# Gated cross-attention and routed experts on one core: Q and K as stacked bf16 parts, select on GpSimd

## What is computed

```
xh = layernorm(x)                                   # per row of 256
Q, K, V = xh @ Wq.T, ctx @ Wk.T, ctx @ Wv.T         # 16 heads of 16 dimensions, 128 queries, 128 keys
scores = where(causal, Q K^T, -inf) / 4
out = softmax(scores) @ V @ Wo.T + bo
x = x + tanh(g0) * out
# then: layernorm, logits, one of 32 tokens per group picked per slot (argmax),
# rows dispatched to 32 experts x 4 sets, relu layer and second layer, combined back
x = x + tanh(g1) * experts(layernorm(x))
```

## Time and profile before

| | |
|---|---|
| median of 3 runs | 319.41 us (316.9 to 321.29) |
| profiled execution, its own time | 319.98 us |
| span of its profile, first to last instruction | 318.2 us |
| around the span | 1.8 us |
| mean granted TensorE clock | 0.93 of full |

### The profile page before, as it was taken

One profiled execution on the slowest core, in us unless ns is written; L12 is line 12 of the kernel. 1 busy time (PEld: TensorE's weight loads), 2 busy tenths in 40 slices (PEclk: granted clock), 3 DMA queues, 4 the chain that ended last, 5 costly groups with the idle time before them and its releaser, 6 DMA issues.

```text
span 318.2 us, 9488 instructions
## 1 busy us (share of the span) xinstructions
PE 286.0 (90%) x3472; PEld 223.0 (70%) x3472; DVE 212.5 (67%) x531; ACT 190.8 (60%) x722; POOL 107.8 (34%) x140
## 2 busy tenths in 40 slices
PE   2195899999999999999999997789988899979995
PEld 2153667778887877777877766667767789867773
DVE  1965997988788887878787984899964233212222
ACT  2035677777777777777777785278764233234553
POOL 4114345544554554455445555145510000000000
PEclk9999999999999999999999997799999755559999
DMA  6992000000000000000000000000005640001222
GB/s 199 369 388 88 2 19 19 19 1 20 16 16 0 16 16 16 0 16 16 13 4 0 0 2 2 0 1 2 0 0 180 214 144 2 6 0 52 72 75 70
DMA packets 12362, 16.52 MB, mean 52 GB/s; under 512 B 1200, under 2 KB 7728, under 8 KB 12336
## 3 DMA queue, kind: packets, MB, share of 16 engines
q1 hardware_dynamic: 11472, 14.83, 14.2%
q10 hardware_dynamic: 864, 1.33, 1.3%
HBM read 14.06 MB, written 2.10 MB: 51 GB/s over the span
## 4 chain that ended last, share of the span: by engine, by line
PE 69%; DVE 13%; SPq 5%; issue 5%; DMA 3%; ACT 3%; POOL 1%; DVEq 0%; ACTq 0%; POOLq 0%
PE banks L351 10%; PE banks L344 9%; PE banks L360 9%; PE banks L562 8%; PE banks L590 7%; PE banks L320 7%; PE banks L330 7%; PE banks L545 4%; DMA cT<-in_ctxT_dram 3%; PE banks L599 3%; PE banks L340 3%; SPq L214 2%; DVE nmax L908 2%; DVE permb L897 2%; PE banks L520 1%
## 5 line engine op out<-in xcount | busy, mean ns | idle before, releaser
L673 ACT ACTIVATE pr<-banks,nmax 128x128 f32<-128x128 f32 x256 | 90.5, 369 | 24.0 <-PE banks L351 17.3
L261 POOL TENSOR_TENSOR pr<-pr,rsum 128x512 f32<-128x512 f32 x64 | 66.6, 1041 | 92.3 <-DVE rsum L857 92.1
L344 PE MATMUL banks<-kd,qz 128*32 128x128 f32 (+3 forms) x512 | 66.9, 437 | 0.0
L360 PE MATMUL banks<-pT,va 128*32 128x128 f32 x512 | 62.0, 276 | 1.7 <-ACT pT L638 1.3
L908 DVE TENSOR_REDUCE nmax<-banks 128x4 f32<-128x512 f32 x64 | 44.0, 687 | 19.5 <-PE banks L344 18.2
L673 ACT ACTIVATION_READ_ACCUMULATOR pr<-banks,nmax 128x1 f32 x256 | 53.2, 208 | 0.0
L360 PEld LDWEIGHTS banks<-pT,va 128*32 128x32 f32 x512 | 38.3, 110 | 17.5 <-DVE pT L870 2.6
L351 PE MATMUL banks<-cf,pr 128*128 128x128 f32 x256 | 42.4, 289 | 1.6 <-POOL pr L261 1.5
L351 PEld LDWEIGHTS banks<-cf,pr 128*128 128x128 f32 x256 | 27.1, 141 | 15.4 <-issue 11.5
L638 ACT ACTIVATE pT<-banks 128x512 f32<-128x512 f32 x32 | 19.2, 599 | 18.5 <-PE banks L351 18.5
L562 PE MATMUL banks<-hb,wx 32*128 32x64 f32 x512 | 27.4, 377 | 2.1 <-ACT hb L751 1.0
(11 more groups left out here) (89 smaller groups left out, 525.2 us busy)
## 6 DMA issues: line engine op xcount, KB each, us to landing
wx<-in_wexp_dram SPq DMA_DIRECT2D x32, 256.5 KB, 5.9
cT<-in_ctxT_dram SPq DMA_DIRECT2D x16, 128.0 KB, 2.1
xs<-in_x_dram SPq DMA_DIRECT2D x4, 512.0 KB, 10.7
out_dram<-xs SPq DMA_DIRECT2D x16, 128.0 KB, 1.7
w<-in_wattn_dram ACTq DMA_DIRECT2D x4, 256.0 KB, 8.0
cf<-in_constf_dram ACTq DMA_DIRECT2D x1, 148.0 KB, 5.9
gb<-in_gbo_dram ACTq DMA_DIRECT2D x1, 129.0 KB, 7.9
ctrl_in<-in_ctrl_dram SPq DMA_DIRECT2D x1, 128.0 KB, 10.5
```

What stands on the lines that cost most here:

```text
L261: pool.tensor_tensor(pr[:, c % 2], pr[:, c % 2], rsum[:, c * HC:(c + 1) * HC, None].to_broadcast([P, HC, P]), ALU.mult)\
L344: last = pe.matmul(bs[r, :, 0:(j + 1) * DP], qz[:, k, c // 2, c % 2, r], kd[:, k, c // 2, :, 0:(j + 1) * DP], start=False, stop=True, tile ...
L360: last = pe.matmul(BO[k][j * DP:(j + 1) * DP, o:o + P], va[:, k, c * HC + j, D * (1 - odd):][:, 0:DP], pT[:, c % 2, j * P:(j + 1) * P], st ...
L673: last = act.activation(pr[:, c % 2, j, :], BS[c % 2][:, j * P:(j + 1) * P], ACT.Exp, bias=nmax[:, c * HC + j:c * HC + j + 1], accum_out=p ...
```

## The change

Attention is written anew, and all hardware loops become written-out lists. There is one list of 76 slots; in slot n, PE makes `scores(n)`, `scores_less_max(n - 6)` and `weigh_v(n - 8)`, each other engine has its own steps at fixed slots, and s = n mod 8, g = n div 8. Q and K are made for two batches at once (eight groups g), each projection as six float32r matmuls per half (256 columns). Each result is split into three bf16 parts (ACT: high, DVE: rest, ACT: middle, POOL: low), stored to DRAM, and read back in an order that stacks parts and dimensions into 96 rows, so that one bf16 matmul with 96 rows gives a head's scores. They are made twice: by rows for the maximum, and transposed, with three more rows that hold the negative maximum in three parts against rows of ones. The exponential then needs no bias and gives the transposed probabilities at once; POOL zeroes those above the diagonal; `weigh_v` multiplies by V and by a matrix of ones for the sums; the division comes at the end. The expert weights no longer have a ring: all 32 lie in memory that the attention's buffers leave free, and are loaded when the last residual is done. A few waits were added in routing (`pick`, `spread`). The sizes: LT = 6, LA = 8, STACKS = 3, PARTS = 3, CH = 64, SLOTS_N = 76, CR = 4, VR = 3, PR = 4. The functions that do it:

```diff
 @block.sync
+            def keep_rows(rows, parts, g, mid, low, kept):
+                sp.wait_ge(mid, g + 1)
+                sp.wait_ge(low, g + 1)
+                sp.dma_start(rows[g].rearrange("t r c -> r t c"), parts[:, :, :]).then_inc(kept, 16)
+            def stack(st, rows, g, order, kept, stacked):
+                sp.wait_ge(kept, 16 * (g + 1))
...
+                for lo, hi in order:      # q: (0,3),(0,2),(0,1); k: (0,3),(1,3),(2,3)
+                    n = (hi - lo) * D
+                    sp.dma_start(st[at:at + n, g % STACKS].rearrange("p h b c -> p (h b c)"),
+                                 rows[g, lo:hi].rearrange("t (d h) c -> (t d) (h c)", d=D)).then_inc(stacked, 16)
...
+            keep_k(0); stack_k(0); load_context(2); keep_q(0); stack_q(0)
...
+            sp.wait_ge(x1_ready, NB)
+            for e in range(NE):
+                sp.dma_start(wx[:, e], wexp[e]).then_inc(wx_loaded[e], 16)
 @block.gpsimd
+            def low_part(parts, i, rest, mid, g, mid_ready, ready):
+                pool.wait_ge(mid_ready, g + 1)
+                pool.tensor_tensor(parts[:, i, :], rest[:, :], parts[:, mid, :], ALU.subtract).then_inc(ready, 1)
+            def drop_above(n):
+                pool.wait_ge(p_ready, n + 1)
+                p = pT[:, n % PR, :].rearrange("p (j q) -> p j q", j=HC)
+                pool.affine_select(p, p, [[0, HC], [1, P]], ALU.is_ge, 0.0, base=0, channel_multiplier=-1)\
+                    .then_inc(pz_ready, 1)
+            for n in range(SLOTS_N):
+                if 0 <= n - LT < CH: drop_above(n - LT)
+                if s % 4 == 1: split_out(n // 4 - 3)            # 256 elements
+                if s == 1: low_part(qp, ..., g + 1)             # 512 elements
+                if s == 5: low_part(kp, ..., g + 2)
+                if s % 4 == 2: bias_x(n // 4)
+                if s == 7: context_low(g + 3)                   # 512 elements
 @block.tensor
+            def scores(n):
+                if n >= 2:
+                    pe.wait_ge(max_ready, n - 1)
+                pe.matmul(to[:, :], identb, causal, start=True, stop=False, skip_group_check=True)
+                for j, h in enumerate(idx):
+                    last = pe.matmul(to[:, j * P:(j + 1) * P], qst[0:SROWS, g % STACKS, h, b % 2, :],
+                                     kst[0:SROWS, g % STACKS, h, b % 2, :], start=False, stop=True, ...)
+            def scores_less_max(n):
+                if n % NC == 0:
+                    pe.wait_ge(rows_loaded[b % 2], 48 * (b // 2 + 1))
+                if n >= 2:
+                    pe.wait_ge(p_ready, n - 1)
+                ... four matmuls of kst[0:TROWS] and qst[0:TROWS], 128 columns each
+            def spread_max(b):
+                pe.wait_ge(np_ready, b + 1)
+                pe.matmul(BB[0:PARTS * H, 0:P], npart (128 x 48), identb).then_inc(nT_done, 1)
+            def weigh_v(n):
+                pe.wait_ge(pz_ready, n + 1)
+                for at, kind in ((0, "v"), (E, "ones")):
+                    for j in range(HC):
+                        left = va[...] if kind == "v" else ones[:, window]
+                        last = pe.matmul(BO[b % 2][j * DP:(j + 1) * DP, ...], left,
+                                         pT[:, n % PR, j * P:(j + 1) * P], tile_position=(0, j * DP), ...)
+            for n in range(SLOTS_N):
+                scores_less_max(n - LT); scores(n)
+                if s % 4 == 0: spread_max(n // 4 - 1)
+                weigh_v(n - LA)
+                if s in (1, 2): project_k(g + 2, s - 1, BA)
+                if s % 4 == 0: project_v(n // 4 - 1)
+                if s == 4:
+                    pe.wait_ge(kr_ready, g + 3)
+                    transpose_x(g + 2, BA)
+                if s % 4 == 2: project_out((n - 14) // 4)
+                if s in (6, 7): project_q(g + 2, s - 6, BA)
 @block.scalar
+            def exps(n):
+                act.activation(pT[:, n % PR, :], BT[n % 2], ACT.Exp, scale=float(D) ** -0.5).then_inc(p_ready, 1)
+            def place_max(b):
+                act.wait_ge(nT_done, b + 1)
+                act.activation(nT[:, b % 2, :], BB[0:PARTS * H, 0:P], ACT.Copy).then_inc(nT_ready, 1)
+                act.wait_ge(nT_ready, b + 1)
+                for t in range(PARTS):
+                    act.dma_start(qst[SROWS + t:SROWS + t + 1, ...], nT[t * H:(t + 1) * H, b % 2, :])\
+                        .then_inc(rows_loaded[b % 2], 16)
+            context_high(0); weight_high(K); weight_high(Q); k_high(0); context_high(1); k_mid(0)
+            xT_high(0, BB); q_high(0, bank[4]); k_high(1, bank[5]); q_mid(0); k_mid(1); ...
 @block.vector
+            dve.memset(kst[SROWS:TROWS], 1.0).then_inc(shift_ready, 1)   # 3 x 16 x 2 x 128 a partition
+            def split_max(b):
+                dve.tensor_copy(npart[:, 0, :], m).then_inc(np_step, 1)
+                dve.wait_ge(np_step, 3 * b + 1)
+                dve.tensor_tensor(r, m, npart[:, 0, :], ALU.subtract).then_inc(np_step, 1)
+                ... then a copy of r and a second subtraction, each behind a wait for the one before
+            def weigh_out(b):
+                dve.wait_ge(av_done, NC * (b + 1))
+                dve.reciprocal(rsum[:, :, :], BO[b % 2][:, E:2 * E]...)
+                ... then on = BO[0:E] * rsum
+            (start) memset of kst; normalize_x(0), (1); weight_low(K), (Q); k_rest(0); xT_low(0);
+                    normalize_x(2), (3); q_rest(0); k_rest(1); xT_low(1); q_rest(1); bias times gate;
+                    statistics(XC, NB); all 13 stages of rstd; then the slots
+            for n in range(SLOTS_N):
+                row_max(n)
+                if s % 4 == 3: split_max(n // 4); residual((n - 15) // 4)
+                if s == 0: q_rest(g + 1)
+                if s % 4 == 0: weigh_out(n // 4 - 3)
+                if s in (1, 2): normalize_x(2 * (g + 2) + s - 1)
+                if s == 3: k_rest(g + 2)
+                if s == 5: xT_low(g + 2)
```

More of the change, by code:

```diff
@@ L40 @@
 GROUPS = NB * NG
-RING = 16
 HR = 4
+NG2 = NB // 2
+CH = NB * NC
+LT = 6
+LA = 8
+SLOTS_N = 4 * NB + 12
+PARTS = 3
+SROWS = 6 * D
+TROWS = SROWS + PARTS
+STACKS = 3
+CR = 4
+VR = 3
+PR = 4
 PAIRS = NE // 2
@@ new lines, in project @@
+            def project(to, m, high, low, o, done=None):
+                parts = [(wt[:, m, i, o * P:(o + 1) * P], src[:, :, i, :])
+                         for i in range(KH) for wt, src in ((wh, high), (wh, low), (wl, high))]
+                for q, (stationary, moving) in enumerate(parts):
+                    last = pe.matmul(to[:, o * E:(o + 1) * E], stationary, moving,
+                                     start=(q == 0), stop=(q == len(parts) - 1))
+                if done is not None:
+                    last.then_inc(done, 1)
@@ L823, in _ @@
             dve.memset(warm[:, :], 0.0).then_inc(act_warm, 1)
-            for c in range(2):
-                dve.memset(BS[c][:, :], NEG).then_inc(above_ready, 1)
             statistics(0, XC)
@@ L885, in pick @@
+            def pick(b):
                 dve.wait_ge(lt_ready, b + 1)
@@ L975, in route @@
+            spread(0)
+            dve.wait_ge(stats_ready, NB)
+            def route(b):
+                stages = range(4 * b, min(4 * b + 4, RSTD_STAGES))
+                if b == 4:
+                    rstd_ready()
                 for stage in stages[:2]:
-                    rstd(stage, NB - 4, NB)
-                if left > 2:
+                    rstd(stage, late, NB)
+                if b + 2 < NB:
                     add_ramp(b + 2)
-                if left > 4:
+                if b + 4 < NB:
@@ L1024, in _ @@
+                if b + 2 < NB:
+                    pick(b + 2)
+                if b + 1 < NB:
+                    spread(b + 1)
+            for b in range(NB):
+                route(b)
             for b in range(NB - 2, NB):
```

1070 lines of the change are left out of this document (558 added, 512 removed).

## The result

The changed kernel takes 389.12 us (median of 4, 386.53 to 391.81) against 319.86 for the kernel before on the same chip: ratio 1.218, interval 1.204 to 1.232. The direction was predicted, the size was not: the range ended at 370. The profiled execution took 391.81 us with a span of 390.0.

What follows compares the result with a forecast made beforehand. PE bounded attention before; afterwards the loop through the maximum would, with DVE and PE close below. Forecast: 190.4 + 15P - G, with P = 11.0 and G = 13, gives 342.4 us; range 317 to 370.

Steps and rivals of the forecast that it cites:

- first row maximum: Start of attention: a chain through DVE, with a memset of 12.8 us, puts it at 53.0 us, 32.6 later than before.
- P: Time of one batch in attention's steady state: 11.0 us taken, bounds 8.6 and 13.1.
- to the end of the last residual: End of attention, from `scores_less_max(60)` through select, `weigh_v`, `weigh_out`, output and residual: 11.6 us.
- G: Expert stage: 13 us back from the clock, as no weights load there and neither pause nor fall was expected.
- the loop through the maximum: Attention: 7.1 us from row maximum to landed rows plus 4.0 of PE work, so at least 11.1 us a batch.
- Both hidden: Attention: POOL with 7.7 us a batch, up to 11.8, and ACT with 6.2 were taken not to bound.
- once a batch: Sign that the forecast is right: `scores_less_max` waits for the rows' DMA one time in each batch of attention.
- `split_max`: Four dependent DVE steps in the loop, slowed by a busy POOL: 0.6 us each, 2.4 a batch, up to 4.4.
- The stacks ... hidden: Stack transfers in attention: 2.4 MB per two batches, in six slots between last part and need, cost nothing.
- PE 9.3 us a batch: Sum of PE's work per batch in attention, 8.6 to 10.4 by other prices, against 10.76 before.
- B: Rival: the clock falls all the same, in attention or the experts, G = 0, 355.4 us; chance 0.20.
- C: Rival: nearly full port waits in `split_max`, 4.0 of at most 4.4, P = 12.7, 368 us; chance 0.10.

Runs made afterwards that it cites:

- e5: Changed kernel without the loads of the Q and K stacks from the fourth pair of batches on; 370.9 us, ratio to before 1.136 to 1.160.
- e2: Changed kernel with the residual ahead of the row maximum in slots holding row maximum, split_max and residual; 380.0 us, ratio to before 1.175 to 1.205.
- e3: Changed kernel with a batch's three transfers of the rows of the maximum made one DMA; 368.9 us, ratio to before 1.137 to 1.156.
- e15: e10 with the rows of ones written by ACT, ctrl_sb awaited before the first logits, statistics ahead of q_rest(1); 325.6 us, ratio to before 1.007 to 1.026.
- e4: Changed kernel with the reciprocal of the row sums replaced by a copy of the same elements; 371.1 us, ratio to before 1.132 to 1.155.
- e8: Kernel before without the second load of 16 experts' weights, so experts 16 to 31 run on the first 16; 310.7 us, ratio 0.972.
- e10: Changed kernel with the four edits, and scores less maximum, exponentials, select and weigh_v one slot later; 333.6 us, ratio to before 1.039 to 1.056.
- the forced 1.69: Kernel before without second expert loads, PE made to wait for a DVE reciprocal ahead of the fifth expert; executions 310.4, 314.9, 322.4 and 323.3 us.
- four edits: Changed kernel with memset on GpSimd, residual ahead of row maximum, one DMA for the maximum's rows, out_high behind the exponential; 361.9 us, ratio 1.106 to 1.128.

## Why the prediction was wrong, step by step

| step | predicted | measured | difference |
|---|---|---|---|
| first row maximum | 53.0 | 56.0 | +3.0 |
| from there to `scores_less_max(0)` | 9.3 | 10.6 | +1.3 |
| 15 x P | 15 x 11.0 | 15 x 12.66 | +24.9 |
| to the end of the last residual | 11.6 | 16.6 | +5.0 |
| G | 13 | 0 | +13.0 |
| sum | 342.4 | 389.6 | +47.2 |

The profiled execution has 391.8; 2.2 us are left to routing and expert stage.

**Two steps failed in P: terms of the loop through the maximum, and "Both hidden" for ACT and POOL.** The measured pair of batches has 27.57 us for 22.2 by the prediction's loop (twice 7.1 + 4.0). Of these 5.4 us, 2.0 lie in the loop through the maximum and 3.4 in the part from 144.24 to 162.70, which took 18.5 for 15.1 and in which PE did not wait for the rows. `scores_less_max` waits for them in every second batch there, not "once a batch".

In the loop, predicted was 7.1 from row maximum to rows; in the chain above it is 171.81 - 162.70 = 9.1. `split_max` was priced too high (it took 1.4, not 2.4). Too low was the transfer: three issues and a landing, priced 3.3 (0.33 each and 2.1 from the DMA of rows 9, and 0.2 for the stacks), took 171.81 - 166.03 = 5.8. Rows 9 are SyncE's issues of a load of another form, with nothing beside it; ACT's of a few small rows took 0.61. And "The stacks ... hidden" asked only whether the stacks come in time, not who stands behind them: e5 gives 18.5 us for that. Left out was the residual in front of `spread_max` (0.6 in the chain; e2's 6.2 us in all is one profile's figure).

In the other part, left out was what is queued behind the issues on ACT: the prediction had added them to the loop and to ACT's busy time and called ACT hidden; e3 gives 17.6 us for a third of their number. This part of the chain runs over ACT, DVE, ACT, POOL and PE, one waiting for the other, and ACT and POOL were "hidden" by busy time alone.

**PE and reciprocal were sized nearly right.** PE 9.3 us a batch: e15 has 147.0 from the first to the last of the 64 maxima, 9.33 for four, at a clock of 0.97. PE is busy for 88% of it, 8.2 us, so that the agreement of 9.3 and 9.33 is in part luck. The reciprocal was put at 1.9 and took 1.75; the estimate from the repeat count in the Trainium skill (VectorE: DVE Perf Modes, First, the fixed hardware budget) was 2.1, and the measurement decides. But its weight is not its length alone: the copy in its place took 11.4 us off the stretch, and the select, 0.64 for a predicted 1.04, cost 16 by what it did to others. The memset was priced 12.8 by the distance of starts; from the end of the instruction before it to its own end it is 12.9, of which its row has 10.3 and 2.6 stand as issue.

**The start** was right within 3 us by its chain, ended by DVE's statistics and the inverse deviation as predicted. The 3 us are there by the statistics' start, 48.3 for 45.1: `q_rest(1)` came late, and the bias took 1.2 for 0.3 behind a wait of 0.9. PE's wait of 8.30 us for ctrl_sb, which the prediction did not name, lay beside it.

**The end**, 5.0 us longer, was not taken apart; e4 shortens it by 4.5 (last row maximum to last residual 23.4 and 18.9), so the reciprocal weighs there too.

**G** is the third step that failed, 13 us for nothing. Its size was a little too high: 8 to 12 us between profiles with and without the fall, and 9.4 in e8. Its condition, no loads beside the stage and so neither pause nor fall, was only half right. With the loads the clock was low each time (all 39 executions of the kernel before that ran beside the experiments have a mean clock between 0.919 and 0.939); without them the fall comes in some executions. The changed kernel's profile has it, with a pause of 1.09 us; its four executions have mean clocks of 0.856 to 0.880. What decides is open: the seven profiles with the fall early in the stage have a pause of PE of 0.95 to 1.52 us there, behind the first experts; nine of the eleven without it have none above 0.82, but two, e10 with 1.10 and the forced 1.69, had the pause and no fall.

Of the rivals B (355.4) had the clock right, and C (P = 12.7) the size of P for the wrong reason: the port waits of `split_max` are 0.48 us a batch, not 3.3. The two together, 190.4 + 190.5 = 380.9, were never added up; the range was built as if only one of them could come.

## What to carry to other kernels

When a wait is added to a loop, price the whole way round it under the loop's own conditions: the issuing engine, what is queued behind the issue on that engine, and which large transfers are issued just before the small one that is waited for. An engine that is busy a third of the time (ACT: 64.8 of 193.2 us) is not hidden if the chain crosses it several times in order; a slot more of distance (23 us here, on top of four edits) or one merged transfer (18 us) was worth more than the reciprocal left out (11 us). And look for the part of a change that pays alone: here it was the place and time of the expert weights, 2.7% without the rest.

## What the runs showed of the hardware that was not expected

- A GpSimd memset of 10.33 us over three partitions holds a DVE instruction of four elements for 5.24 us, after three two-input ones of the same size had run beside it in 0.16 to 0.17 each; work moved to an idle GpSimd can still be paid by DVE.
- The rows of the maximum, 4 to 12 KB within SBUF, land 1.7 us after their issue at best, and 4.4 to 5.4 us after it when three loads of 128 to 384 KB were issued around 1 us ahead of it, from another queue.
- Three issues of 16 rows cost ACT 1.79 us, one of 48 rows 0.73.
- The clock in attention was 1.00 with PE busy 97% of the time, 0.89 with 74% (changed) and 0.98 with 88% (e15: 129.2 of 146 us). Which part of the longer stretches is the clock's own was not separated.
- The clock of the expert stage differs from one execution to the next of one kernel, worth 8 to 12 us. No profile had an early fall without a pause of at least 0.95 us, but two had such a pause and no fall.
